# Spectral filter products as two 64-column tiles, one per token parity, and evictions over all 128 rows

## The reference, cut to what matters

```python
def _stu_conv(phi, u, n):                    # u: (b, sl, d), phi: (L, K)
    sgn = jnp.where(jnp.arange(sl) % 2 == 0, 1.0, -1.0)
    Vf = jnp.fft.rfft(phi, n=n, axis=0)
    Uf_p = jnp.fft.rfft(u, n=n, axis=1)
    Uf_m = jnp.fft.rfft(u * sgn[None, :, None], n=n, axis=1)
    U_plus = jnp.fft.irfft(Vf[None, :, :, None] * Uf_p[:, :, None, :], n=n, axis=1)[:, :sl]
    U_minus = jnp.fft.irfft(Vf[None, :, :, None] * Uf_m[:, :, None, :], n=n, axis=1)[:, :sl]
    return U_plus, U_minus * sgn[None, :, None, None]
...
out = jnp.einsum('btkd,k,kde->bte', U_plus, s, Mpp)
out = out + jnp.einsum('btkd,k,kde->bte', U_minus, s, Mpm)
out = out + _compute_ar_u(Mu, u)             # three taps
```

## Time and profile before

| | us |
|---|---|
| median of 3 runs | 1365.69 (1363.75 to 1367.94) |
| the profiled execution | 1374.82 |
| its span | 1372.2 |
| PE busy | 1258.2 (92% of the span) |
| ACT busy | 638.8 (47%) |
| DVE busy | 606.5 (44%) |
| the spectral stage's loop | about 488 (715 to 1203) |

### The profile page before, as it was taken

One profiled execution on the slowest core, in us unless ns is written; L12 is line 12 of the kernel. 1 busy time (PEld: TensorE's weight loads), 2 busy tenths in 40 slices (PEclk: granted clock), 3 DMA queues, 4 the chain that ended last, 5 costly groups with the idle time before them and its releaser, 6 DMA issues. The chain is left out here.

```text
span 1372.2 us, 29519 instructions
## 1 busy us (share of the span) xinstructions
PE 1258.2 (92%) x12746; PEld 841.1 (61%) x12746; DVE 606.5 (44%) x1008; ACT 638.8 (47%) x1217; POOL 190.3 (14%) x206
## 2 busy tenths in 40 slices
PE   8999989888888799999879999999999999988766
PEld 5223328777777678888756655665565556566544
DVE  3992114112111567777543434443343434456643
ACT  2996754324567545455453333433344334332430
POOL 4100003950000422222131001000100000002000
PEclk9988999999999799999979999999999999989968
DMA  5900000000000240000050000000000000050002
GB/s 114 126 1 1 1 1 5 1 1 1 1 1 1 65 109 4 4 4 4 3 138 9 9 1 1 9 9 1 1 16 1 1 1 1 1 124 1 1 1 62
DMA packets 46205, 28.57 MB, mean 21 GB/s; under 512 B 28253, under 2 KB 44701, under 8 KB 46077
## 3 DMA queue, kind: packets, MB, share of 16 engines
q1 hardware_dynamic: 45693, 25.63, 9.1%
q10 hardware_dynamic: 384, 1.07, 0.3%
HBM read 22.37 MB, written 2.21 MB: 18 GB/s over the span
## 5 line engine op out<-in xcount | busy, mean ns | idle before, releaser
L1311 DVE TENSOR_TENSOR sp_sums<-sp_y,sp_shared 64x512 f32<-64x512 f32 (+1 forms) x256 | 176.3, 689 | 263.5 <-ACT sp_shared L1286 237.7
L1282 ACT COPY sp_sums<-sp_y 64x512 f32<-64x512 f32 x256 | 148.5, 580 | 241.5 <-PE sp_y L1177 236.6
L1177 PE MATMUL sp_y<-hankel,sp_ut 128*128 128x256 f16 x768 | 125.7, 273 | 0.0
L1244 PE MATMUL sp_o<-sp_sums,mix 128*64 128x128 f32 (+2 forms) x1024 | 122.8, 390 | 0.0
L1163 PE MATMUL sp_y<-hankel_sum,sp_ut 128*128 128x512 f16 x384 | 104.9, 383 | 0.0
L1163 PE MATMUL sp_y<-hankel,sp_ut 128*128 128x512 f16 x384 | 104.5, 381 | 0.3 <-ACT sp_sums L1282 0.3
L1174 PE MATMUL sp_y<-hankel,sp_late 128*128 128x256 f16 x512 | 98.0, 273 | 0.3 <-DMA sp_late<-sp_ut 0.3
L503 PE MATMUL convv<-runningv,toeplitz 128*128 128x128 f32 x610 | 83.8, 284 | 12.6 <-DVE runningv L523 12.6
L503 PE MATMUL convh<-runningh,toeplitz 128*128 128x128 f32 x610 | 84.1, 283 | 8.1 <-DVE runningh L523 8.1
L1174 PEld LDWEIGHTS sp_y<-hankel,sp_late 128*128 128x128 f16 x512 | 48.3, 98 | 65.0 <-issue 18.7
L1244 PEld LDWEIGHTS sp_o<-sp_sums,mix 128*64 128x64 f32 x1024 | 64.2, 134 | 38.0 <-issue 27.4
(11 more groups left out here) (333 smaller groups left out, 2149.9 us busy)
## 6 DMA issues: line engine op xcount, KB each, us to landing
hankel<-phi_rows SPq DMA_DIRECT2D x32, 160.0 KB, 3.0
hankel_sum<-phi_rows SPq DMA_DIRECT2D x32, 128.0 KB, 3.3
ex_w<-in_L_ffn_weight SPq DMA_DIRECT2D x1, 2080.0 KB
m_plus<-in_L_ffn_M_phi_plus SPq DMA_DIRECT2D x2, 1024.0 KB, 14.1
m_minus<-in_L_ffn_M_phi_minus SPq DMA_DIRECT2D x2, 1024.0 KB, 16.6
sp_late<-sp_ut SPq DMA_DIRECT2D x32, 64.0 KB, 2.1
out<-x SPq DMA_DIRECT2D x8, 256.0 KB, 3.3
x<-in_x ACTq DMA_DIRECT2D x2, 512.0 KB, 7.9
```

The source lines that it names most:

```text
L1177: mm = nc.tensor.matmul(out[:, :, P:SPAN], ut[g % 2][:, hu, b, s, :, :].rearrange("p a c -> p (a c)"), m.hankel[:, hf, some, P:SPAN], star ...
L1244: mm = nc.tensor.matmul(out_of(lo, cnt, par), m.mix[:, 2 * j + n, SCALES - 1 - seg, par, :], sums[:, n, :, lo + par:lo + cnt:2], start=Fal ...
L1282: nc.scalar.copy(sums[HALF[a], :, b, to], y_ps[r][HALF[a], :, of]).then_inc(y_c[r], 1)
L1311: nc.vector.tensor_tensor(sums[HALF[a], :, b, to], y_ps[r][HALF[a], :, of], shared[done % 2][HALF[a], :, of], op).then_inc(y_c[r], 1)
```

## The change

The stationary operand is split by parity: each matmul of `product` and `first_block` becomes two of 64 columns, one for `a` = 0 into rows 0 to 63 of the bank and one for `a` = 1 into rows 64 to 127. Each reads the table at its own offset, `lo + 1 - a`, so that the shift by one token is in the product. The banks can then be evicted over all 128 rows at once with one range of tokens: L1282 and L1311 are one instruction for a bank where they were two, and the semaphore counts follow. The zero for the first token and `first_ok` go. The table starts one element earlier and its rows are one element longer (769 for 768, 513 for 512), so half of the float16 reads of the table start at an odd element.

```diff
+CORNER = P + 1
...
-        def summed(r, a):
-            lo = r * SPAN + a
-            hi = min(lo + SPAN, T)
-            return slice(lo, hi), slice(0, hi - lo)
+        def summed(r):
+            return slice(r * SPAN, (r + 1) * SPAN)
...
                     for n, (hu, hf) in enumerate(PRODUCTS):
-                        mm = nc.tensor.matmul(out[:, :, :], ut[g % 2][:, hu, b, s, :, :].rearrange("p a c -> p (a c)"),
-                                              table[:, hf, 2 * j:2 * j + 2, lo:lo + SPAN],
-                                              start=first and n == 0, stop=last and n == len(PRODUCTS) - 1, skip_group_check=True)
+                        for a in range(2):
+                            mm = nc.tensor.matmul(out[HALF[a], :, :], ut[g % 2][:, hu, b, s, a, :],
+                                                  table[:, hf, 2 * j:2 * j + 2, lo + 1 - a:lo + 1 - a + SPAN],
+                                                  start=first and n == 0, stop=last and n == len(PRODUCTS) - 1, skip_group_check=True)
...
                     for piece in range(PIECES16):
+                        for a in range(2):
+                            nc.tensor.matmul(out[HALF[a], :, 0:P + a], late[g % 2][:, piece, b, s, a, :],
+                                             m.hankel[:, 0, some, 1 - a:CORNER], start=opens and piece == 0, stop=piece == 1, skip_group_check=True)
                     for n, (hu, hf) in enumerate(PRODUCTS):
+                        for a in range(2):
+                            mm = nc.tensor.matmul(out[HALF[a], :, P + a:SPAN], ut[g % 2][:, hu, b, s, a, :],
+                                                  m.hankel[:, hf, some, CORNER:CORNER + P - a], start=False, stop=n == len(PRODUCTS) - 1, skip_group_check=True)
...
-                        taken(y_c[r], 2)
+                        taken(y_c[r], 1)
...
-                pe.wait_ge(first_ok, 1)
...
-                                for a in range(2):
-                                    to, of = summed(r, a)
-                                    nc.scalar.copy(sums[HALF[a], :, b, to], y_ps[r][HALF[a], :, of]).then_inc(y_c[r], 1)
+                                nc.scalar.copy(sums[:, :, b, summed(r)], y_ps[r][:, :, :]).then_inc(y_c[r], 1)
...
-                nc.vector.memset(sums[HALF[1], :, :, 0:1], 0.0).then_inc(first_ok, 1)
...
-                                for a in range(2):
-                                    to, of = summed(r, a)
-                                    nc.vector.tensor_tensor(sums[HALF[a], :, b, to], y_ps[r][HALF[a], :, of], shared[done % 2][HALF[a], :, of], op).then_inc(y_c[r], 1)
+                                nc.vector.tensor_tensor(sums[:, :, b, summed(r)], y_ps[r][:, :, :], shared[done % 2][:, :, :], op).then_inc(y_c[r], 1)
...
-            sp.dma_start(m.hankel[:, piece, k, P:NEAR], whole).then_inc(m.table_in, 16)
+            sp.dma_start(m.hankel[:, piece, k, CORNER:], whole).then_inc(m.table_in, 16)
-        corner = bass.AP(phi_rows.tensor, late, [[2, C], [1, P]])
+        corner = bass.AP(phi_rows.tensor, late, [[2, C], [1, CORNER]])
...
-            src = bass.AP(phi_rows.tensor, (k * PIECES16 + piece) * PHI_ROW + SPAN + NEAR + 2, [[2, P], [1, 2 * SPAN]])
+            src = bass.AP(phi_rows.tensor, (k * PIECES16 + piece) * PHI_ROW + SPAN + NEAR + 1, [[2, P], [1, 2 * SPAN + 1]])
```

More of the change, by code:

```diff
@@ L1076, in spectral_stage @@
         o_ps = pb("sp_o", [P, 2, 2, T // 4])
-        (u_ok, apart_ok, ar_set, zero, ut_ok, ut_hi, ut_c, p_ok, p_c, ar_ok, mix_ok, o_c, first_ok) = (sem("st_" + n) for n in (
-            "u", "apart", "taps_stacked", "zeroed", "ut", "ut_high", "ut_taken", "shared", "shared_taken", "ar_done", "mixed", "added", "first"))
+        (u_ok, apart_ok, ar_set, zero, ut_ok, ut_hi, ut_c, p_ok, p_c, ar_ok, mix_ok, o_c) = (sem("st_" + n) for n in (
+            "u", "apart", "taps_stacked", "zeroed", "ut", "ut_high", "ut_taken", "shared", "shared_taken", "ar_done", "mixed", "added"))
         late_in = [sem(f"st_late_in{k}") for k in range(2)]
@@ L1233, in mixed @@
                     pairs = g * KP + j + 1
-                    pe.wait_ge(y_c[0], 4 * pairs)
-                    pe.wait_ge(y_c[1], 4 * pairs)
+                    pe.wait_ge(y_c[0], 2 * pairs)
+                    pe.wait_ge(y_c[1], 2 * pairs)
                     for some in ((2, 1, 0), (3,)):
                         if some == (3,):
-                            pe.wait_ge(y_c[2], 4 * pairs)
-                            pe.wait_ge(y_c[3], 4 * pairs)
+                            pe.wait_ge(y_c[2], 2 * pairs)
+                            pe.wait_ge(y_c[3], 2 * pairs)
                         for n in range(2):
@@ L2069, in hankel_load @@
     for k in range(FILTERS):
-        first = k * PIECES16 * PHI_ROW + SPAN - 2 * (P - 1)
+        first = k * PIECES16 * PHI_ROW + SPAN - 2 * (P - 1) - 1
         late = first + 2 * C
         for piece in range(PIECES16):
-            whole = bass.AP(phi_rows.tensor, first + piece * PHI_ROW + P, [[2, P], [1, NEAR - P]])
-            sp.dma_start(m.hankel[:, piece, k, P:NEAR], whole).then_inc(m.table_in, 16)
-        corner = bass.AP(phi_rows.tensor, late, [[2, C], [1, P]])
-        sp.dma_start(m.hankel[HALF[1], 0, k, 0:P], corner).then_inc(m.table_in, 16)
-        corner_low = bass.AP(phi_rows.tensor, late + PHI_ROW, [[2, C], [1, P]])
-        sp.dma_start(m.hankel[HALF[0], 0, k, 0:P], corner_low).then_inc(m.table_in, 16)
+            whole = bass.AP(phi_rows.tensor, first + piece * PHI_ROW + CORNER, [[2, P], [1, NEAR + 1 - CORNER]])
+            sp.dma_start(m.hankel[:, piece, k, CORNER:], whole).then_inc(m.table_in, 16)
+        corner = bass.AP(phi_rows.tensor, late, [[2, C], [1, CORNER]])
+        sp.dma_start(m.hankel[HALF[1], 0, k, 0:CORNER], corner).then_inc(m.table_in, 16)
+        corner_low = bass.AP(phi_rows.tensor, late + PHI_ROW, [[2, C], [1, CORNER]])
+        sp.dma_start(m.hankel[HALF[0], 0, k, 0:CORNER], corner_low).then_inc(m.table_in, 16)
 def hankel_sum_load(nc, m, phi_rows, sp):
@@ L2138, in hybrid_program @@
                 sb, pb, sem = open_pools(nc, filters)
-                m.hankel = sb("hankel", [P, PIECES16, FILTERS, NEAR], F16)
+                m.hankel = sb("hankel", [P, PIECES16, FILTERS, NEAR + 1], F16)
                 with ExitStack() as ctx:
@@ L2149, in hybrid_program @@
                 sb, pb, sem = open_pools(nc, filters)
-                m.hankel_sum = sb("hankel_sum", [P, PIECES16, FILTERS, 2 * SPAN], F16)
+                m.hankel_sum = sb("hankel_sum", [P, PIECES16, FILTERS, 2 * SPAN + 1], F16)
                 spectral_norm_stage(nc, m, phi_rows)
```

6 lines of the change are left out of this document (1 added, 5 removed).

## The result

Twenty runs of each kernel: before 1368.16 us in the median, after **1363.96 us**. The ratio is 0.9968, 95% interval [0.9954, 0.9982]: a gain of 4.2 us between the medians, 0.32%, right at the edge of what can be told from no change; the interval reaches from 2.5 to 6.3 us. The forecast was 6.5 us. Half of that is the starting point: the 20 runs of before lie 2.5 us higher in the median than the 3 that the forecast started from (1365.69).

The account below looks back on a forecast made before the run. PE's distance between starts was taken to bound the loop; -1.0 (evictions) + 0.4 (widths) - 5.9 (switches) = -6.5 us, from the median 1365.7 to 1359.2 us. The forecast's own range was 1357 to 1362, with rivals 1356 to 1378.

Parts of the forecast that it names:

- What bounds the kernel: In the stage's loop PE is busy 487.0 of 488.0 us, so the distance between PE's starts counts.
- Evictions, -1.0: Half as many evictions on ACT and DVE remove two waits at the loop's start, 0.7 + 0.3 us: -1.0 us.
- Switches, -5.9: Fewer changes between 128*128 and 128*64 tiles around `mixed` and `autoregressive`, less new ones after turns: together -5.9 us.
- +0.15 for the new switch: Nine new tile-shape switches from the turn's transposes to `filtered`, each priced at 0.15 us: 1.35 us in all.
- Weight loads, 0: Two 64-column loads for each pair hide behind the matmuls: 0; if exposed, up to 134 us.
- The table's DMAs, 0: Longer, odd-starting table rows stay hidden: 0; a rival with doubled load and `late` 10 us later had chance 0.03.
- The pair's distance: In `filtered`, 2240 split pairs start as far apart as full-width matmuls, 0.216 or 0.109 us: 0, other end 17.0 us.
- +0.4 for the widths: In `late` the odd half streams 258 columns instead of 256, in 512 pairs of 0.84 ns: +0.4 us.
- the 4.9% of `mixed`: Pairs in `mixed`, reading every second element, start 0.45 us apart against 0.429 full width; not expected in the new products.
- the second rival: A surcharge of 1 to 4 ns a pair from twice as many instructions, 2 to 9 us, about 1365; chance 0.18.
- the first rival: Two streams cost what they do in `mixed`, through odd starts or neighbouring addresses: +10.5 us, 1376; chance 0.26.
- The nearest row, L203: Float32 pairs at L203, same tiles and 512 contiguous columns, start 0.43 us apart, nothing extra; basis for taking 0.

Follow-up runs that it names:

- tiles_only: Kernel before with each product matmul split into two 64-column tiles reading the same table elements, evictions, table and widths as before; loop 481.7 us, ratio 0.9958.
- product_only: Kernel before with only the 512-column matmuls of `product` split into two 64-column tiles, `first_block` kept full width; loop 530.3 us, one run 1414.6 us.
- parity_sums: Changed kernel with `sums` stored by parity: evictions read PSUM with a step of two, `mixed` reads contiguously; loop 477.8 us, 1356.69 us, ratio 0.9914.
- unequal: tiles_only with the changed kernel's unequal widths alone, 128 + a and 128 - a columns for each filter; loop 483.2 us, one run 1364.6 us.
- far_streams: tiles_only with the odd half reading another pair of filters, 1536 elements away in `hankel`, 1024 in `hankel_sum`; loop 481.7 us, one run 1363.0 us.
- odd_same: Changed kernel with both halves reading at `lo + 1`, equal widths, rows of 770 elements, every read starting odd; loop 484.4 us, one run 1365.4 us.

## Why the prediction was wrong, point by point

- **What bounds the kernel: right.** PE's distances between starts set the loop, before and after. The 160 us of work that ACT and DVE shed are worth 1.3 us.
- **Evictions, -1.0: right in place, somewhat too small.** The waits went as said, all in the first cycle, and one for `late` with them: -1.3 us.
- **Switches, -5.9: right in mechanism and sum.** tiles_only shows 5.8 us over 31 cycles and product_only that it is the shape. Its parts: a plain cycle gains 14.715 - 14.474 = 0.24 us where 0.26 was worked out; a cycle with a turn goes from 15.297 to 15.240, where +0.15 for the new switch was to cancel the -0.15 of the old one, so the new one costs less: with 0.11 for the way back, a plain cycle's 0.24 leaves 0.13 for the old one, and 0.13 - 0.06 = 0.07 for the new; its row above shows 0.09. That the sum came out so well is partly luck: the plain cycles gain 0.3 us less than forecast in all, and the cycles with a turn 0.4 us more.
- **Weight loads, 0: right.** They take 109 ns and two to a pair, and tiles_only's pairs are as close as full-width ones.
- **The table's DMAs, 0: right.** `late` is not waited for any more.
- **The pair's distance, "and I take 0", with +0.4 for the widths: this step failed.** It measures +2.8 us, 0.087 us in a cycle of 70 pairs, or 1.2 ns a pair. It is not the 4.9% of `mixed`, which went when its step of two did, as the forecast had it (parity_sums, with the reservation there). It is the second rival by size, "a small surcharge of 1 to 4 ns", but not by its reason: twice as many instructions cost nothing (tiles_only). The reason is nearer to that of the first rival, at a sixth of its 17 us. It comes with where the float16 reads start, how the two streams stand to each other, and the widths, for which, as the forecast said of the first two, the trace of before had no row. The widths alone measure +1.5 us (unequal). The forecast had counted the two columns more in `late` and taken the other pairs as "no longer than before"; in fact the odd half has two columns fewer there (254), and yet the time that it lost is not made good. The nearest row, L203, has neither an odd start nor a displacement, and so could not carry a 0 here.

By terms: -5.8 - 1.3 + 2.8 = -4.3 us, against 4.2 both in the loop and in the medians of the runs. The forecast had -5.9 - 1.0 + 0.4 = -6.5.

Open stays how the 2.8 us divide, and why the tiles of a pair drift apart when their widths differ or their streams lie one or two elements apart.

## What to carry to other kernels

Where TensorE bounds a kernel, read the distances between starts and look for places where the tile shape changes; giving all matmuls of a loop one shape saved 0.1 us at each, and halving the instructions of engines that wait saved almost nothing. A matmul whose moving operand is strided may be paying for it in each instruction: let the evictions, which have time, do the reordering, as parity_sums did for more than the change itself brought. When a term is "a few ns times thousands" and no row shows the operation, don't take the round zero but an amount within its bounds, and measure a loop from its own first start to its own last, since the rest of the span scatters by more than what is looked for.

## What the runs showed of the hardware

- Two column tiles of float16 run side by side at the full-width pace, 0.216 us for 512 columns and 0.109 for 256, even with 109 ns a load (tiles_only) and with streams 1024 and 1536 elements apart (far_streams).
- A switch between 128*128 and 128*64 costs 0.114 us in the mean over product_only's twelve a cycle, in either direction and within one type.
- float16 reads of the moving operand that start at an odd element cost about 1.9 ns for a pair, with 512 columns as with 256: 0.218 for 0.216 and 0.111 for 0.109 us (odd_same; its table rows were two elements longer as well).
- The two tiles of a pair can drift apart: with 258 and 256, then 254 and 256 columns the second fell behind by 40 ns in a cycle of 70 pairs, and after the next transposes it was back at 3 ns (unequal).
- A float32 moving operand with a step of two, the two tiles one element apart, costs 4.9%: 0.450 against 0.429 us for 512 columns (`mixed` in after and in parity_sums).
- ACT reads PSUM with a step of two at no cost (587 ns), DVE for 10 ns (701 against 691).
